# Loop bodies set at the head of an instruction fetch block, with a prefetch hint for the back edge

## What is computed

```python
xn = layernorm(x)
# graph attention, 4 heads: for each edge exp(leaky_relu(a_src[src] + a_dst[dst]) - m[dst]),
# normalised over the edges of a target, times h[src], summed by target (and a self edge)
gnn = relu(layernorm(gat(xn, src, dst) + bias + xn) * gamma + beta)
# linear attention, 8 heads, over all nodes, then a second rmsnorm
h = xn + linear_attention(rmsnorm(xn)) @ w_out + b_out
x = x + gnn + h + rmsnorm(h) * w_norm2
# 8 experts, the 2 best of each node, hidden size 512
x = x + moe(layernorm(layernorm(x)) * gamma + beta)
```

## Time and profile before

| what | us |
|---|---|
| median of 3 runs | 5643.91 |
| lowest, highest | 5628.12, 5650.48 |
| profiled execution, its own time | 5658.8 |
| span of the profiled execution | 5656.9 |

### The profile page before, as it was taken

How to read it: one execution, slowest core, us unless ns; L and a number is a source line. 1 busy time by engine, 2 the same in 40 slices (tenths; PEclk the granted TensorE clock), 3 DMA queues, 4 the chain that set the end, 5 groups by cost and what they waited for, 6 DMA issues and landing times. The chain is left out here.

```text
span 5656.9 us, 82461 instructions
## 1 busy us (share of the span) xinstructions
PE 3141.8 (56%) x17248; PEld 2519.1 (45%) x17249; DVE 2765.0 (49%) x6991; ACT 1170.5 (21%) x3323; POOL 2594.0 (46%) x2690
## 2 busy tenths in 40 slices
PE   4997055455555555555566655540034300599998
PEld 3775034343344444444444544430023200599998
DVE  6554234344444444444555677778832400255554
ACT  2443011111111111111111211113322100133332
POOL 3000166666666666666666422224400066444444
PEclk9998577777777777777777766665555555799999
DMA  4111743434344343333333333333311143344443
GB/s 134 57 57 56 223 111 105 105 102 107 103 105 108 101 107 101 104 97 103 102 103 105 87 93 90 93 91 121 122 45 37 41 163 115 86 71 70 71 71 59
DMA packets 414267, 540.74 MB, mean 96 GB/s; under 512 B 70588, under 2 KB 355212, under 8 KB 414078
## 3 DMA queue, kind: packets, MB, share of 16 engines
q0 software_dynamic: 114496, 265.49, 19.2%
q1 hardware_dynamic: 252014, 226.39, 14.4%
q10 hardware_dynamic: 47728, 48.55, 2.6%
HBM read 395.58 MB, written 145.82 MB: 96 GB/s over the span
## 5 line engine op out<-in xcount | busy, mean ns | idle before, releaser
L996 POOL DMA_INDIRECT rows<-node_rows,index x1564 | 1656.7, 1059 | 928.7 <-issue 467.1
L1135 PE MATMUL ps_sum<-msg,hot 128*128 128x260 f32 x3904 | 1238.1, 472 | 908.4 <-DVE big L1077 742.3
L1135 PEld LDWEIGHTS ps_sum<-msg,hot 128*128 128x128 f32 x3904 | 866.6, 234 | 1075.3 <-issue 603.4
L1068 DVE TENSOR_TENSOR msg<-rows,msg 128x1024 f32<-128x1024 f32 x488 | 600.3, 1230 | 81.8 <-ACT msg L1096 63.8
L1050 DVE TENSOR_REDUCE e<-ps_tgt 128x32 f32<-128x96 f32 x488 | 122.9, 252 | 987.3 <-remote 930.0
L1086 ACT ACTIVATE hot<-ps_hot 128x512 f32<-128x512 bf16 x488 | 291.4, 597 | 1280.3 <-remote 787.1
L1841 POOL DMA_INDIRECT out_dram<-big,x_rows x204 | 352.4, 1727 | 438.4 <-DVE big L1933 390.9
L1867 PEld LDWEIGHTS x_ps_hT<-x_rowsT,x_w_now 128*128 128x128 f32 x3264 | 398.8, 193 | 11.5 <-DVE x_w_now L1911 1.1
L1867 PE MATMUL x_ps_hT<-x_rowsT,x_w_now 128*128 128x128 f32 x3264 | 399.8, 276 | 0.7 <-DVE x_w_now L1911 0.7
L1114 PE MATMUL ps_hot<-ident_h,hotT 128*128 128x128 bf16 x1952 | 217.4, 241 | 308.3 <-DVE hotT L1044 159.5
L1876 PE MATMUL x_ps_out<-w,x_actT 128*128 x1632 | 385.9, 379 | 0.0
(11 more groups left out here) (269 smaller groups left out, 4994.6 us busy)
## 6 DMA issues: line engine op xcount, KB each, us to landing
targets<-dst_row SPq DMA_DIRECT2D x391, 128.0 KB
expert_in<-c_blank ACTq DMA_DIRECT2D x51, 520.0 KB
x_rows<-expert_in SPq DMA_DIRECT2D x204, 130.0 KB
rows<-node_rows,index POOLq DMA_INDIRECT x1564
node_rows<-h_out SPq DMA_DIRECT2D x98, 132.0 KB
h_row<-node_rows SPq DMA_DIRECT2D x98, 132.0 KB
queries<-q_out SPq DMA_DIRECT2D x98, 128.0 KB
q_in<-queries SPq DMA_DIRECT2D x98, 128.0 KB
```

The source lines that it names most:

```text
L996: g.indirect_dma_start(rows[:, j, k, :], None, s.node_rows, bass.IndirectOffsetOnAxis(ap=index[:, b, j * G + k:j * G + k + 1], axis=0)).th ...
L1068: v.tensor_tensor(m[:, :, 0:D].rearrange("p g (h f) -> p g h f", h=GH), rows[:, bass.ds(here, 1), :, 0:D].rearrange("p j g (h f) -> p (j g ...
L1135: mm = pe.matmul(ps_sum[:, j % 2, 0:SUM], hot[:, j % MSGS, k * P:(k + 1) * P], msg[:, j % MSGS, k, :], start=(k == 0), stop=(k == G - 1))
```

## The change

```diff
+def loop(eng, first, end, step=1):
+
+    return eng.bass.Fori(first, end, step, engines=[eng.engine], hint_back_edge=True, head_slot={eng.engine: 0})
+
+
 def in_step(eng, steps, lag, count, head, ring):
...
-    with eng.Fori(0, (count - head) // ring) as i:
+    with loop(eng, 0, (count - head) // ring) as i:
...
                 for j in range(7):
                     v.wait_ge(x_in[j], 16 if j < 6 else 32)
-                    with v.Fori(14 * j, 14 * (j + 1) + (j == 6)) as t:
+                    with loop(v, 14 * j, 14 * (j + 1) + (j == 6)) as t:
...
-                with g.Fori(1, LOOPS) as i:
+                with loop(g, 1, LOOPS) as i:
...
-                with v.Fori(0, TILES - 1, 2) as t0:
+                with loop(v, 0, TILES - 1, 2) as t0:
```

More of the change, by code:

```diff
@@ L270, in _ @@
                 sp.sem_inc(store_free, 2)
-                with sp.Fori(0, TILES - 1, 2) as t0:
+                with loop(sp, 0, TILES - 1, 2) as t0:
                     for u in range(2):
@@ L429, in _ @@
                 copy_rT(0, 0)
-                with act.Fori(0, TILES - 1, 2) as t0:
+                with loop(act, 0, TILES - 1, 2) as t0:
                     for u in range(2):
@@ L457, in _ @@
                 transpose_r(0, 0)
-                with pe.Fori(0, TILES - 1, 2) as t0:
+                with loop(pe, 0, TILES - 1, 2) as t0:
                     for u in range(2):
@@ L606, in _ @@
                                     base=0, pattern=[[1, P]], channel_multiplier=-1).then_inc(masked, 1)
-                    with g.Fori(0, COLS // 2) as i:
+                    with loop(g, 0, COLS // 2) as i:
                         for u in range(2):
@@ L624, in _ @@
                 with pe.If(faulty(pe, s, 0) != 0):
-                    with pe.Fori(0, COLS) as c:
+                    with loop(pe, 0, COLS) as c:
                         pe.wait_ge(hot_ready, c + 1)
@@ L646, in one_hot @@
                         v.tensor_scalar(hot[:, :], s.row_iota[:, :], window[:, bass.ds(c, 1)], None, ALU.is_equal).then_inc(hot_ready, 1)
-                    with v.Fori(0, COLS) as c:
+                    with loop(v, 0, COLS) as c:
                         one_hot(c)
@@ L692, in _ @@
                         place_chunk(c, c, 0, done + STEPS * c)
-                    with v.Fori(1, COLS // 2) as i:
+                    with loop(v, 1, COLS // 2) as i:
                         for u in range(2):
@@ L820, in _ @@
                     table = s.src_table.rearrange("(p c) o -> p (c o)", p=P)
-                    with sp.Fori(0, PAIRS) as n:
+                    with loop(sp, 0, PAIRS) as n:
                         past = sp.value_load(plan.entry[0:1, bass.ds(n, 1), 2], min_val=1, max_val=SUPERS)
@@ L830, in _ @@
                 with g.If(faulty(g, s, 1) != 0):
-                    with g.Fori(0, PAIRS) as n:
+                    with loop(g, 0, PAIRS) as n:
                         g.wait_ge(edges_in, n * 32 + 32)
@@ L840, in _ @@
                 with pe.If(faulty(pe, s, 1) != 0):
-                    with pe.Fori(0, PAIRS) as n:
+                    with loop(pe, 0, PAIRS) as n:
                         pe.wait_ge(wide_ready, n + 1)
@@ L851, in _ @@
                     v.tensor_copy(peaks[:, :, :], s.scores[:, :, 0:GH]).then_inc(folded, 1)
-                    with v.Fori(0, PAIRS) as n:
+                    with loop(v, 0, PAIRS) as n:
                         w = v.value_load(plan.window[0:1, bass.ds(n, 1)], min_val=0, max_val=WINDOWS - 1)
@@ L972, in _ @@
                     track(m, m, m // RING)
-                with sp.Fori(1, LOOPS) as i:
+                with loop(sp, 1, LOOPS) as i:
                     for m in range(UNROLL):
@@ L1207, in load @@
                     sp.dma_start(x_row[0:rows, u, :], x[bass.ds(t * P, rows), :]).then_inc(loaded[u], 16)
-                with sp.Fori(0, TILES - 3, 2) as t0:
+                with loop(sp, 0, TILES - 3, 2) as t0:
                     load(t0, 0, P)
@@ L1218, in _ @@
                 g.wait_ge(w_in, 48)
-                with g.Fori(0, TILES - 1, 2) as t0:
+                with loop(g, 0, TILES - 1, 2) as t0:
                     for u in range(2):
@@ L1246, in _ @@
                 tile(1, 0, 1, False)
-                with act.Fori(2, TILES - 1, 2) as t0:
+                with loop(act, 2, TILES - 1, 2) as t0:
                     tile(t0, t0, 0, False)
@@ L1399, in _ @@
                 load(1, 1, P)
-                with sp.Fori(2, TILES - 3, 2) as t0:
+                with loop(sp, 2, TILES - 3, 2) as t0:
                     for u in range(2):
@@ L1608, in _ @@
                 centre(1, 1)
-                with act.Fori(0, TILES - 3, 2) as t0:
+                with loop(act, 0, TILES - 3, 2) as t0:
                     for u in range(2):
```

## The result

The changed kernel takes 5708.0 us (median of 4 runs, 5681.65 to 5715.0) where the kernel before took 5645.73 us in the runs beside it: ratio 1.0112, 95% interval 1.0089 to 1.0135. The forecast was 5686 us, with 5640 to 5715 as its range; the result lies near the upper end.

What follows compares the result with a forecast made beforehand. No single engine bounds the kernel; the bound differs by stage, and no loop refetches its body. Hints 15.8 us plus entries 26.8 us make 42.6, on 5643.9 us: 5686 us, range 5640 to 5715.

Steps and rivals of the forecast that it cites:

- The entries: Waits for one fetch at each entry to a placed loop and at the skipped stages: 26.8 us, from 0 to 40.
- the loops' terms: Hint cost per turn in the statistics loops, combine, route and attend_edges, with join at 0: 15.8 us, from 0 to 27.
- No fetch to take away: All loops: 29 instruction packets against 379 VectorE turns, so no loop refetches its body and the hint has no stall to remove.
- The hint's price, 70 ns: Each exposed turn: one more sequencer instruction, 70 ns, the middle of 40 and 98; L349 6.9 us, combine and route 3.4 each.
- `attend_edges`, 2.1 us: Hint in attend_edges: 60 VectorE turns at 70 ns, 4.2 us, half counted because VectorE is only sometimes on the path.
- `join`, 0: Hint and placement in join's 49 turns: saving of at most 0.06 us against a hint of 0.07 us, sum set to 0.
- the bound of 0.06 us: Idle time at join's back edge, taken as the most that placement can save per turn, 3 us over 49 turns.
- The price of an entry, 2.2 us, at most 2.7: Entering a placed loop two pieces on waits for one fetch; the seven L349 loops on VectorE make 15.4 us.
- Skipped stages, 4.4 us: sort_by_window and shift_by_target: jumps over their padded loops cost 2.2 us each ahead of a barrier.
- First tiles of the tile loops, 6 us for four: attend_edges, combine, join, route: entry waits of 1.5 us each, partly beside another engine's start; project's is covered, 0.
- `scatter_rows` 1, experts 0: Entries in the last stages: half of one in scatter_rows, 1 us; none in run_experts, where TensorE is full.
- The first: Rival for placed loops: the next head is fetched ahead, entries cost 0, hint 15.8 us; 5660 us, no change; chance 0.34.

## Why the prediction came out as it did

Its mechanism was right and its sum too low: 42.6 us were forecast, and the medians differ by 5708.0 - 5645.7 = 62.3. That the range held is in part luck. The entries, at most 40 us by the forecast, came to 30.1 + 6.1 + 8.8 = 45.0 us without those of the last two stages; the loops' terms, at most 27 us, stayed at 8.0 + 9.4 - 2.1 + 4.0 = 19.3.

- **No fetch to take away.** Right. The branch of L354 is no quicker with the hint (61 ns, 56), and the hint alone makes the kernel 0.5% slower.
- **The hint's price, 70 ns.** 81 in L349's loops, 77 in `route`, 80 in `combine`. L349 8.0 us for 6.9, `route` 4.0 for 3.4, `combine`'s own part 4 for 3.4. Its record of 39 ns understates it; my middle of 40 and 98 was too low by a seventh. `combine` lost 9.4 in all, the rest with a lower clock, for which the forecast had no term. The other engines' hints cost nothing in `combine`, as said, and `project` and `run_experts` hide theirs.
- **`attend_edges`, 2.1 us.** Not shown. Plain loops there give nothing back, and the stage itself moves by more than that: from first to last gather it took 2566.2 us in the run with VectorE's hint in `combine`, whose code in this stage is that of the kernel before, at 2584.2.
- **`join`, 0.** The step that failed is the bound of 0.06 us for what placement can save there. It took only the idle before the product. But inside a turn the product starts 0.35 us after the statistics, before these end, so by the same rows the edge costs 0.49 - 0.35 = 0.14 us. Placement alone took 0.10 of it, 3.9 us in the loop. With the hint the gain was 2.1 us in the changed kernel's trace; five traces with the same code in `join` have 315.6 to 317.8 us for 317.7, so the net gain is somewhere from 0 to 2 us.
- **The price of an entry, 2.2 us, at most 2.7.** This is the term that was mis-sized, and its upper bound was too low as well. It is 2.9 us, and 6.1 when it begins under full load. I bounded it by `w_ext` (2.7), a data transfer that is asked for by a running program. I also reasoned that the loads didn't matter because the statistics ran evenly; they mattered to the fetches. Seven entries: 15.4 forecast; 6.9 of the later first start and 79.0 - 47.8 - 8.0 = 23.2, so 30.1 us.
- **Skipped stages, 4.4 us.** 6.1, of the length of one fetch each, 3.25 and 2.84 us.
- **First tiles of the tile loops, 6 us for four.** 8.8 for three (3.1, 2.7, 3.0), so not halved by overlap. In `join` the cover that I counted on, ScalarE's start, was itself late, since ScalarE's loop was placed as well. `attend_edges` hid its own: from L1017 to the first addition of a sum (L1082) it is 103.1 us, and 103.2 before. `project` hid its own too: VectorE waits 1.74 us for TensorE before the first `k_exp` where it waited 4.57.
- **`scatter_rows` 1, experts 0.** 2.8 together; no run takes them apart.
- **The rivals.** The first is right about heads at the next piece and wrong about these. The Trainium skill, "Runtime: NRT & Kernel Launch", section "Instruction fetch mechanics", gives blocks of 16 KiB (256 instructions). By that the head of each statistics loop would have been in the next block, and found there. The trace disagrees for VectorE, and the measurement decides: 2.9 us to enter a head two multiples of 128 on, 0.5 us for the next one. The same section says that a taken branch out of the window stalls; with that the traces agree, at 2.9 to 3.5 us.

## What to carry to other kernels

A loop's head may be moved only as far as the next piece that the fetch ahead brings, which costs 0.5 us an entry, and only for a loop that lies across a boundary; a head one piece further costs 3 us at every entry, twice that while data is loading. Short loops entered many times on a chain of one engine are the worst place for it. A hint per turn costs some 80 ns of the sequencer, so before adding one, look for fetches at back edges in the number of instruction packets. Where the edge is exposed, fewer and longer turns save more than any placement, as long as the body isn't fetched anew each turn: bodies of 212 and 214 instructions were not, one of 373 was, and nothing between was measured.

## What the runs showed of the hardware

- The pieces of VectorE's code that are fetched ahead hold 128 instructions, 8 KB, one piece ahead. A jump over one of them is a fetch on demand of 2.9 us with the DMA engines idle, 6.1 us when it begins at 345 GB/s. The packet itself takes 0.3 to 0.6 us either way; what grows is the time until it starts (0.8 and 3.9 us). I had expected one size for all conditions. The jump to the next piece takes 0.5 us.
- A branch prefetch hint's record is 39 ns on VectorE, and it delays the turn by 77 to 81 ns.
- A body that lies across a piece's boundary, as far as is inferred here, costs about 80 ns an edge (`join`, 3.9 us in 49). From the start of its closing branch to the next instruction it was 287 ns, and 191 behind the placement.
- A body of 373 instructions paid 3.5 us at every back edge, bodies of 212 and 214 nothing of the kind.
- One step of `combine` takes 5.8 us at a granted clock of 0.50 and 4.8 at 0.86, so that the same code in this stage took 564 to 569 us.
- One chip ran the kernel before in 5274 us, others in 5639 to 5682; there the gathers of the two versions with 14 tiles a turn took 2211 and 2214 us from first to last, in the version with 8 tiles in `combine`, on another chip, 2542.
